# An attention and FFN kernel in split fp32r: the product with the moving low part goes last in each group, and three steps change places in their queues

## The reference, cut to what matters

```python
# x, ctx: (8, 512, 2048).  C = 512 channels, D = 2048, 8 groups of 64 channels
def xattn(q, k, v):                  # q = layernorm(x), k = v = ctx
    t, p, g = Wt @ v, Wp @ q, Wg @ k
    att = sum over a group's 64 x 2048 values of p * g
    y = blockdiag(Wz) @ (att * t)
    return groupnorm(y) * gn_w + gn_b + v
def ffn(x):                          # x: (4096, 2048), columns permuted by perm
    for each head h of 16 (128 columns each):
        out_h = gelu(t_h @ up[h]) @ down[h]          # 128 -> 512 -> 128
    return the columns put back
x = x + xattn(layernorm(x), ctx, ctx)
x = x + ffn(layernorm(x))
```

## Time and profile before

| | |
|---|---|
| median of 3 runs | 1542.35 us (1542.32 to 1544.04) |
| the profiled execution's own time | 1544.83 us |
| its span in the trace | 1543.0 us |
| PE busy | 1504.6 us (98%), 6592 matmuls |
| DVE, ACT, POOL busy | 1193.9, 1067.2, 957.0 us |
| DMA | 374.8 MB, mean 243 GB/s |

### The profile page before, as it was taken

The page is one execution under the profiler, slowest core; times in us unless marked ns, Lnnn a source line. Parts: engine busy times, 40 slices in busy tenths (PEclk is TensorE's granted clock), DMA queues, the critical chain, the costliest instruction groups (busy, mean ns, idle before and its releaser), DMA issues.

```text
span 1543.0 us, 19537 instructions
## 1 busy us (share of the span) xinstructions
PE 1504.6 (98%) x6592; PEld 1235.2 (80%) x6592; DVE 1193.9 (77%) x1514; ACT 1067.2 (69%) x1321; POOL 957.0 (62%) x765
## 2 busy tenths in 40 slices
PE   8899998998999999999999999999999999999998
PEld 7677887886888888888888888878888888877786
DVE  5888866865788767877778876787778876889786
ACT  4445847763886748875687856878478774899776
POOL 1482576177881738726586267843578355898887
PEclk9999999999999999999999999999999999999999
DMA  8987787877577845778467793767847676758886
GB/s 326 358 320 270 255 261 281 293 224 250 178 270 257 256 138 198 266 252 277 129 213 243 267 276 120 237 239 248 261 134 262 243 245 209 237 195 255 265 289 218
DMA packets 166867, 374.79 MB, mean 243 GB/s; under 512 B 14960, under 2 KB 80496, under 8 KB 158576
## 3 DMA queue, kind: packets, MB, share of 16 engines
q1 hardware_dynamic: 141424, 281.25, 55.6%
q0 software_dynamic: 25344, 92.29, 16.9%
HBM read 287.45 MB, written 86.03 MB: 242 GB/s over the span
## 4 chain that ended last, share of the span: by engine, by line
PE 69%; POOL 9%; DVE 8%; DMA 7%; issue 4%; ACT 2%; SPq 1%; POOLq 0%; ACTq 0%; DVEq 0%
PE PP L863 19%; PE PP L877 17%; PE PP L931 14%; PE PP L916 13%; PE PP L890 5%; POOL FB L1310 3%; POOL FB L1313 3%; DVE R L1058 2%; DMA RAW<-in_cx 2%; POOL out L1318 2%; POOL FB L1295 2%; DMA FB<-xg_scratch,perm_sb 1%; DMA WW<-w_scratch 1%; DVE R L1223 1%; DMA RAW<-in_Wg 1%
## 5 line engine op out<-in xcount | busy, mean ns | idle before, releaser
L916 PE MATMUL PP<-GG,WW 128*128 128x512 f32 x1536 | 391.6, 391 | 7.6 <-DVE GG L1218 5.0
L863 PE MATMUL PP<-R 128*128 128x512 f32 x1536 | 354.8, 391 | 8.6 <-DVE R L1058 7.5
L877 PE MATMUL PP<-R,WC 128*128 128x512 f32 x1536 | 352.2, 391 | 7.7 <-ACT Z L972 7.7
L916 PEld LDWEIGHTS PP<-GG,WW 128*128 128x128 f32 x1536 | 288.4, 189 | 72.2 <-issue 11.0
L863 PEld LDWEIGHTS PP<-R 128*128 128x128 f32 x1536 | 289.3, 189 | 69.4 <-issue 7.9
L877 PEld LDWEIGHTS PP<-R,WC 128*128 128x128 f32 x1536 | 289.7, 189 | 69.0 <-ACT Z L972 8.5
L931 PE MATMUL PP<-R,WW 128*128 128x512 f32 x1050 | 270.5, 393 | 6.5 <-DMA WW<-w_scratch 3.9
L1020 ACT ACTIVATE PP<-PP 128x1024 f32<-128x1024 f32 x256 | 261.8, 1023 | 0.0
L1223 DVE TENSOR_TENSOR R<-PP,R 128x1024 fp32r<-128x1024 f32 x175 | 213.6, 1220 | 60.4 <-ACT PP L1020 60.0
L1019 ACT ACTIVATE R<-PP 128x1024 fp32r<-128x1024 f32 x175 | 180.0, 1029 | 104.0 <-PE PP L916 103.9
L1302 POOL TENSOR_TENSOR X<-X,RAW 128x512 f32<-128x512 f32 x112 | 189.3, 1722 | 96.5 <-DVE bn L1043 84.2
(11 more groups left out here) (96 smaller groups left out, 1609.7 us busy)
## 6 DMA issues: line engine op xcount, KB each, us to landing
WW<-w_scratch SPq DMA_DIRECT2D x152, 512.0 KB
X<-in_x SPq DMA_DIRECT2D x32, 1024.0 KB, 5.6
RAW<-in_cx SPq DMA_DIRECT2D x32, 1024.0 KB
RAW<-in_xT SPq DMA_DIRECT2D x63, 512.0 KB
RAW<-in_cT SPq DMA_DIRECT2D x63, 512.0 KB
xg_scratch<-FB SPq DMA_DIRECT2D x104, 256.0 KB
w_scratch<-WW POOLq DMA_DIRECT2D x16, 1024.0 KB, 6.0
HX<-wp_scratch SPq DMA_DIRECT2D x7, 1024.0 KB, 8.2
```

What stands on the lines that cost most here:

```text
L863: t = eng.matmul(s_bank(c1), l[:, part(c1)], r, start=(dt == 0 and j == 0), stop=(dt == ND - 1 and j == 2))
L877: t = eng.matmul(PP[2 + ot // 2][:, ot % 2, :], WC[:, l, ct, part(ot)], u[:, r + ct, :], start=(ct == 0 and j == 0), stop=(ct == NT - 1 an ...
L916: t = eng.matmul(PP[slot["up", f, p]][:, e, :], wt[:, l, part(2 * p + e)], g[:, r, :], start=(j == 0), stop=(j == 2))
```

## The change

- **The products' order.** In every group of three the product whose moving operand is the low part comes last, and the wait for that part stands just ahead of it. In `y_mm`, `v_mm`, `up_mm` and `dn_mm` all products with the moving high part come first (8 of 12 in `y_mm` and `v_mm`, 4 of 6 in the others). `s_mm` is split in two steps: `s_hh` (high x high, one matmul) and `s_mm` (the other two); for batches 0 and 1, and for chunks 4 to 15 later, the four `s_hh` of a chunk come ahead of its four `s_mm`. The wait for a free PSUM bank goes with `s_hh`.
- **Wp's parts stored later.** `keep_wp` is due at 21.5 rather than 9.5.
- **Batch 2's first chunks loaded later.** `load_s(2, 0..2)` are due 13, 10 and 7 units ahead of S of batch 2, where it was 15.2, 14.4 and 13.
- **The gathers of batch 2.** Its first three are due 2.4 units ahead of V, where it was 3.6.

```diff
-    put(9.5, keep_wp)
+    put(21.5, keep_wp)
...
-            put(s0 + ((-15.2, -14.4, -13)[j] if i == 2 and j < 3 else S_LOAD[j] if i > 1 else (-14, -10, -8)[j] if i and j < 3 else 2 * j - (5 if i or j else 10)), load_s, i, j)
+            put(s0 + (S_LOAD[j] if i > 1 else (-14, -10, -8)[j] if i and j < 3 else 2 * j - (5 if i or j else 10)), load_s, i, j)
...
-                put(s0 + (dt + 0.25 * c1 if i < 2 or dt > 3 else S_EARLY[c1 // 2][dt][c1 % 2]), s_mm, i, dt, c1)
+                whole = i < 2 or dt > 3
+                put(s0 + (dt + 0.08 * c1 if whole else S_EARLY[c1 // 2][dt][c1 % 2]), s_hh, i, dt, c1)
+                put(s0 + (dt + 0.34 + 0.16 * c1 if whole else S_EARLY[c1 // 2][dt][c1 % 2]), s_mm, i, dt, c1)
...
-            put(v0 - 3.6 + 0.1 * g if i < 3 and g < 3 else max(lead - 6.5, v0 - 3 if g == 0 else v0 - 1), gather, f, b, h)
+            put(v0 - (3.6 if i < 2 else 2.4) + 0.1 * g if i < 3 and g < 3 else max(lead - 6.5, v0 - 3 if g == 0 else v0 - 1), gather, f, b, h)
...
                 pe.wait_ge(*at["ghi", f])
+                pe.wait_ge(*at["w", w, 0])
+                g, wt, pp = G[f % 2], WW[w % 2], PP[slot["up", f, p]]
+                for e in range(2):
+                    for l in range(2):
+                        eng.matmul(pp[:, e, :], wt[:, l, part(2 * p + e)], g[:, 0, :], start=(l == 0), stop=False)
                 pe.wait_ge(*at["glo", f])
-                pe.wait_ge(*at["w", w, 0])
-                g, wt = G[f % 2], WW[w % 2]
                 for e in range(2):
-                    for j, (l, r) in enumerate(((1, 0), (0, 1), (0, 0))):
-                        t = eng.matmul(PP[slot["up", f, p]][:, e, :], wt[:, l, part(2 * p + e)], g[:, r, :],
-                                       start=(j == 0), stop=(j == 2))
+                    t = eng.matmul(pp[:, e, :], wt[:, 0, part(2 * p + e)], g[:, 1, :], start=False, stop=True)
```

More of the change, by code:

```diff
@@ L132, in s_lo, with s_hh, s_mm @@
         order.append(("s_lo", i, dt))
-    def s_mm(i, dt, c1):
+    def s_hh(i, dt, c1):
         if dt == 0:
             free["sb", i, c1] = take(("PP", c1 // 2, c1 % 2))
+        order.append(("s_hh", i, dt, c1))
+    def s_mm(i, dt, c1):
         t = n.up("smm", i, dt, c1)
@@ L852, in tensor @@
                         t.then_inc(S["wc"], 1)
-            elif stage == "s_mm":
+            elif stage == "s_hh":
                 i, dt, c1 = a
                 pe.wait_ge(*at["shi", i, dt])
-                pe.wait_ge(*at["slo", i, dt])
-                xh, ch = s_tile(i, dt, 0)[:, 0, :], s_tile(i, dt, 0)[:, 1, :]
-                xl, cl = s_tile(i, dt, 1)[:, 0, :], s_tile(i, dt, 1)[:, 1, :]
                 if dt == 0:
@@ L861, in tensor @@
                         pe.wait_ge(*t)
[L862 to L865, removed]
+                hi = s_tile(i, dt, 0)
+                eng.matmul(s_bank(c1), hi[:, 0, part(c1)], hi[:, 1, :], start=(dt == 0), stop=False)
+            elif stage == "s_mm":
+                i, dt, c1 = a
+                pe.wait_ge(*at["slo", i, dt])
+                hi, lo = s_tile(i, dt, 0), s_tile(i, dt, 1)
+                eng.matmul(s_bank(c1), lo[:, 0, part(c1)], hi[:, 1, :], start=False, stop=False)
+                eng.matmul(s_bank(c1), hi[:, 0, part(c1)], lo[:, 1, :], start=False,
+                           stop=(dt == ND - 1)).then_inc(S["smm"], 1)
             elif stage == "y_mm":
@@ L872, in tensor @@
                 pe.wait_ge(*at["yhi", i, q])
+                u = R[slot["y", i, q]]
+                for l in range(2):
+                    for ct in range(NT):
+                        eng.matmul(PP[2 + ot // 2][:, ot % 2, :], WC[:, l, ct, part(ot)], u[:, ct, :],
+                                   start=(l == 0 and ct == 0), stop=False)
                 pe.wait_ge(*at["ylo", i, q])
-                u = R[slot["y", i, q]]
                 for ct in range(NT):
-                    for j, (l, r) in enumerate(((1, 0), (0, 4), (0, 0))):
-                        t = eng.matmul(PP[2 + ot // 2][:, ot % 2, :], WC[:, l, ct, part(ot)], u[:, r + ct, :],
-                                       start=(ct == 0 and j == 0), stop=(ct == NT - 1 and j == 2))
+                    t = eng.matmul(PP[2 + ot // 2][:, ot % 2, :], WC[:, 0, ct, part(ot)], u[:, 4 + ct, :],
+                                   start=False, stop=(ct == NT - 1))
                 t.then_inc(S["ymm"], 1)
```

27 lines of the change are left out of this document (17 added, 10 removed).

## The result

| | before | changed |
|---|---|---|
| median, same chip | 1542.34 us (4 runs, 1542.28 to 1544.04) | 1526.26 us (4 runs, 1523.13 to 1529.37) |
| ratio of the times | | 0.9893, 95% interval 0.9867 to 0.9919 |
| the profiled execution, its span | 1544.83, 1543.0 us | 1524.07, 1522.2 us |

So that the first median fell 0.24 us outside says little; what the prediction got wrong is in its terms.

The account below looks back on a forecast made before the run. The prediction took PE as the bound, at an unchanged matmul rate, with gains only from its stands and half clock. Its terms summed to -11.7 us: 1530.6 us against the median of 1542.35, range 1526.5 to 1539.5.

Parts of the forecast that it names:

- rival 5: All of PE's matmuls: the new interleaving costs PE rate, slower by over 0.2%, 1550 us at 3 ns each; chance 0.05.
- rival 1: Batch 0: Wp's store isn't through by 84.8 and delays row sums and V, up to 5 us, 1535.6 us; chance 0.12.
- DVE's whole sequence moves up by at most 5.07 us: Batch 0: DVE becomes the bound, gaining at most its two waits of 1.90 and 3.17 us; batch 0 gains 5.9 us.
- The 0.9 us by which S was to end earlier: Batch 0, last chunk of S: four of twelve matmuls done before the low part arrives, so S ends 0.9 us earlier.
- the forecast 3.5 us: Batch 0, ahead of V: PE's wait grows from 1.84 to 3.5 us.
- The 1.7 us: Batch 0, V: half clock after the longer wait costs +1.7 us, bounds 0 and 2.8.
- The border: Start of S of batch 1: six matmuls no longer cover the wait for the last bank, +1.4 us.
- FFN of batch 1: Later chunk loads remove the weights' stand of 3.62 us, its half clock and the 1.26 us: -6.6 us.
- rival 2: FFN of batch 1: weights late again one head on, a stand of 1 to 3.6 us, about 1535 us; chance 0.12.
- Two slots' worth of time hide it: FFN of batch 1: about 5 us per weight half hide the other two chunk loads, at most 1.5 MB (3.6 us).
- V and FFN of batch 2: Gathers start 2.8 us later behind head 7 and its wait for head 5's store: +0.4 us, half clock stays.
- The small waits: Four matmuls cover each low-part wait: -1.5 us in batches 3 to 6, -1.2 us in the last batch.

Follow-up runs that it names:

- again_changed: The changed kernel run once more in another session, nothing altered: 1529.28 us (8 runs), ratio 0.9919 to the kernel before.
- evacuate_first: Changed kernel with batch 2's correction and split of S due 0.6 units later, behind Z's evacuations: 1534.35 us, ratio 0.9935 to the kernel before.
- best_parts: Changed kernel with batch 1's first S chunk bank by bank, batch 2's evacuations ahead of S's corrections, its gathers back ahead of head 7's split: 1526.13 us.
- without_products: Changed kernel with the old order of products, the three queue moves kept: 1535.01 us, ratio 0.9941 to the kernel before.
- only_keep_wp: Kernel before with Wp's store due at 21.5 alone: 1533.61 us, ratio 0.9937 to the kernel before.
- without_products_and_gathers: Kernel before with only Wp's store and batch 2's chunk loads moved: 1529.76 us, ratio 0.9917 to the kernel before.
- pair_at_border: Changed kernel with the first chunk of S of batch 1 ordered bank by bank again: 1525.06 us, ratio 0.9891 to the kernel before.
- without_gathers: Changed kernel with the gathers of batch 2 back at their old place: 1527.88 us, ratio 0.9903 to the kernel before.
- without_keep_wp: Changed kernel with Wp's store back at 9.5, ahead of ctx's blocks: 1536.89 us, ratio 0.9952 to the kernel before.

## Why the prediction was wrong, point by point

- **Where the time would come from was right.** Wp's store was the largest part (0.63% alone), and its mechanism and first number were right too (split of block 1 at 65.65 for 65.5). PE's rate did not change: Y of batch 3 takes 43.52 us for 192 matmuls before and after, so rival 5 fell, and with it the rule of the Trainium skill ("TensorE: Matmul & The Clock Gate", section "A second HAM failure mode: psum-queue depth-cycling") as a threat to this kernel: `s_hh` changes the bank with every matmul and the rest of S with every second, and still twelve matmuls of S take 2.72 us (226.7 ns each) and the clock in S, Y and V was 1.00 wherever PE had not stood before. `store_sum` was issued at 82.92, 0.2 us before Wp's second part landed (67.33 + 15.8), and its way took less time than before, so rival 1 fell too.
- **The failed step: "DVE's whole sequence moves up by at most 5.07 us".** It moved by 4.9 us at block 1 and by 7.3 at block 3 (95.48 to 88.17), since its instructions got shorter as POOL fell differently beside them (by the rows above; no run moved POOL alone). The low part of block 3 was there at 90.45, and PE, which reached q = 3 at 90.0, needed it at 91.8: no stand where 2 us were forecast. The way of the row sums, from `store_sum` to the first correction, shrank from 14.5 (89.90 to 104.37) to 11.0 us (82.92 to 93.89), which I had taken as fixed; 2.8 us of that is the load of the sums on all partitions, 8.4 us to landing before and 5.6 after. The 0.9 us by which S was to end earlier didn't come: PE's wait for the last low part ended at 55.39, where it was 54.15. Batch 0 thus gained 10.4 us for 5.9, there was no wait ahead of V for the forecast 3.5 us, and no half clock. With the half clock that is 6.2 us more than the sum had, more than the 4.3 us by which the median fell below the forecast.
- **The half clock was charged to the wrong stand.** The 1.7 us fell behind the 3.02 us in S of batch 1 and behind the 2.00 us in Y of batch 2. The border cost 3.3 us for 1.4: the six matmuls as reckoned, plus the slow clock.
- **FFN of batch 1, 6.6 forecast, 2.7 measured.** The 3.62 us and their half clock went, as reckoned; but rival 2 came in small, three stands of about 1 us behind `w_scratch`, with the moved chunk loads between the weight loads. "Two slots' worth of time hide it" was the step that failed: the three loads that PE waited for took 7.7, 8.9 and 8.2 us to land, where about 5 us of time were granted. The 2.2 us lost in Y of batch 2 were in no term at all.
- **V and FFN of batch 2, -0.4 forecast, +6.9 measured.** I let the gathers wait for head 5's store until 2.8 us past their old time, because I kept POOL where it stood against PE. But the store was now issued 7.1 us ahead of V, not 4.8 (347.12 against 354.19; 357.03 against 361.79), landed after 7.4 us for 7.8, and the gathers left 4.1 us after V, where it had been 4.0. Then they took 3.44 us to the high part, not 4.83, with the quiet queue; the low part 0.69, not 2.08. With four matmuls on the high part ahead, the stand of 3.53 us and its 2.8 us of half clock vanished. The 2.2 us lost in Y and the 6.9 gained here are one matter, since the later V is part of the shorter wait; together they are 4.7 us. Of the 6.9, again_changed kept all but 1.9 us.
- **The small waits, 1.5 + 1.2 forecast, 3.3 + 3.0 measured.** Places and causes were right, the size was not. The rows were miscounted, too: behind 452.23, batches 3 to 6 have four stands of about 0.32 us and not two, beside the one of 0.52, so that the idle time in this term was 2.1 us and not 1.5. A batch in which 0.32 us of idle time is shown and then not, shrank by 0.65 us (186.10 to 185.45 from Y of batch 3 to Y of batch 4). Over batches 3 to 6 five stands of 1.81 us in sum were worth 3.3 us, some 0.3 us each above what the rows show. A row's end includes a matmul's 391 ns, 164 more than its pace of 227; that, and the start of the pipeline, is not counted as idle. The sum over many small stands should carry this.

What stays open: why head 5's store lands after 10.6 to 12.7 us in five profiles (evacuate_first, best_parts, without_products, only_keep_wp, without_products_and_gathers) and after 7.3 to 8.0 in nine others. In four of the five it was issued less than 3.1 us ahead of V, in the nine 4.7 us or more; without_products_and_gathers, with 4.7 us and 10.6, shows that this isn't all. Open too is how often the changed kernel meets the late case. Over all its runs and those of pair_at_border, with the gathers behind head 7, 4 of 18 were above 1531 us; of 16 with the same products and the gathers ahead of it, none. So few runs don't show that the place of the gathers is the reason, and no profile caught such a run.

## What to carry to other kernels

A bulk store that nobody needs soon belongs behind the loads that somebody waits for; here one such line was worth 0.6%, the most of four parts. A moved chain has to be costed with its new neighbours: a DVE instruction took 1.6 us longer and gathers up to 5.1 us longer in other company, more than most terms of the sum. A chain that one engine brings earlier has to be held against the engines that don't come earlier with it: in evacuate_first V of batch 2 came 3 us sooner, POOL's store didn't, and PE stood for 11.35 us. And a step should not stand ahead of an urgent one on an in-order queue if it waits for a store's landing, even if the landing is in time in one profile.

## What the runs showed of the hardware

- PE's clock fell to half after a stand of 2.00 us (Y of batch 2, changed kernel) and stayed whole after one of 2.28 us at the same place in without_gathers. At the border to S of batch 1, 3.02 us had it and 1.67 didn't, and of two stands of 2.44 us there one had it (evacuate_first, clock 0.50) and one didn't (without_keep_wp, clock 1.00). The stand's length alone doesn't decide.
- A stand that the timeline of before shows as 0.32 us (at 638.33) set the starts of the matmuls back by 0.56 us.
- POOL's 1 MB stores of split weights took 4.2 to 12.7 us to land over all profiles, SP's 1 MB stores of Wp's parts 10.9 to 17.4.
